# The shift unit of a graph-transformer layer moved into the last feed-forward quarter, in two groups of tiles

## The reference

```python
xn = layernorm(x)
x = x + gnn(xn) + mixer(xn)       # gnn: 4 experts of 2 graph layers; mixer: 2 attention + feed-forward layers
x = x + shift_unit(layernorm(x))  # last step, row by row:
# y = layernorm(x); hot = y > 0.5
# lo, hi, sa = first hot column of y[64:80], y[80:96], y[96:112] (0 if none)
# val = lo + 16*hi; shl = (val << sa) & 255; shr = val >> sa
# act_shl = hot[0] and hot[39];  act_shr = hot[0] and hot[40] and not hot[39]
# res = shl, shr or 0;  amp = 2 if either is active
# y[128:144] += amp * onehot(res & 15);  y[144:160] += amp * onehot(res >> 4)
```

## Time and profile before

| | us |
|---|---|
| median of 3 runs (lowest to highest) | 1983.43 (1982.74 to 1987.58) |
| the profiled execution's own time | 1988.76 |
| its span | 1986.9 |
| TensorE busy | 1815.1 |
| TensorE's last matmul ends, from the span's start | 1956.5 |
| VectorE's last instruction ends | 1981.9 |

### The profile page before, as it was taken

One profiled execution on the slowest core, in us unless ns is written; L12 is line 12 of the kernel. 1 busy time (PEld: TensorE's weight loads), 2 busy tenths in 40 slices (PEclk: granted clock), 3 DMA queues, 4 the chain that ended last, 5 costly groups with the idle time before them and its releaser, 6 DMA issues. The chain is left out here.

```text
span 1986.9 us, 26833 instructions
## 1 busy us (share of the span) xinstructions
PE 1815.1 (91%) x9484; PEld 1498.1 (75%) x9484; DVE 863.3 (43%) x1777; ACT 646.4 (33%) x1211; POOL 614.2 (31%) x503
## 2 busy tenths in 40 slices
PE   1798999999999999968999989999989998899993
PEld 1455788888888788857788867887877988778883
DVE  8996311111111146455565456222666554552236
ACT  7844211111111211015546523221365465222210
POOL 4003432323241343106321006433361210254432
PEclk9999999999999999989999999999999999999997
DMA  2168512213121567235702001011175020011102
GB/s 62 41 150 135 70 60 94 86 69 127 47 106 42 198 232 195 95 113 147 212 27 95 22 1 42 22 43 46 36 202 155 30 92 22 1 43 43 57 25 65
DMA packets 112174, 166.46 MB, mean 84 GB/s; under 512 B 42712, under 2 KB 60871, under 8 KB 111052
## 3 DMA queue, kind: packets, MB, share of 16 engines
q1 hardware_dynamic: 112067, 165.05, 28.8%
HBM read 103.24 MB, written 55.53 MB: 80 GB/s over the span
## 5 line engine op out<-in xcount | busy, mean ns | idle before, releaser
L774 PE MATMUL ps<-yT,wslot 128*128 128x500 f32 (+1 forms) x576 | 208.3, 362 | 9.5 <-ACT qpT L1790 5.9
L775 PE MATMUL ps<-yT,wslot 128*128 128x500 f32 (+1 forms) x576 | 207.3, 360 | 0.0
L776 PE MATMUL ps<-yT,wslot 128*128 128x500 f32 (+1 forms) x576 | 207.0, 359 | 0.0
L1018 PE MATMUL ps<-g,adj 125*128 125x512 f32 (+1 forms) x800 | 186.3, 394 | 1.4 <-DVEq L1153 1.2
L1018 PEld LDWEIGHTS ps<-g,adj 125*128 125x128 f32 (+1 forms) x800 | 150.2, 188 | 37.5 <-DVEq L1153 1.6
L2152 POOL TENSOR_TENSOR hidT<-qpT,hidT 128x500 fp32r<-128x500 f32 (+1 forms) x96 | 103.3, 1079 | 213.8 <-DVE hidT L1935 213.8
L1790 ACT ACTIVATE qpT<-ps,all_cols 128x500 f32<-128x500 f32 (+1 forms) x96 | 58.1, 610 | 313.8 <-PE ps L776 266.7
L2147 POOL TENSOR_TENSOR wslot<-mix_landing,wslot 128x512 fp32r<-128x512 f32 x92 | 121.8, 1354 | 115.1 <-ACT wslot L1726 115.1
L774 PE MATMUL ps<-parts,w 128*128 128x500 f32 (+1 forms) x384 | 136.0, 354 | 2.2 <-PEq L559 2.2
L775 PE MATMUL ps<-parts,w 128*128 128x500 f32 (+1 forms) x384 | 136.1, 354 | 0.0
L776 PE MATMUL ps<-parts,w 128*128 128x500 f32 (+1 forms) x384 | 136.0, 354 | 0.0
(11 more groups left out here) (295 smaller groups left out, 3686.8 us busy)
## 6 DMA issues: line engine op xcount, KB each, us to landing
mix_landing<-in_L_mix_W SPq DMA_DIRECT2D x16, 1024.0 KB, 5.1
qk_dram<-qk_parts SPq DMA_DIRECT2D x128, 125.0 KB, 2.4
g_dram<-staged SPq DMA_DIRECT2D x40, 256.0 KB, 2.0
u_dram<-staged SPq DMA_DIRECT2D x40, 256.0 KB, 2.0
g_in<-g_dram SPq DMA_DIRECT2D x40, 256.0 KB, 3.6
u_in<-u_dram SPq DMA_DIRECT2D x40, 256.0 KB, 2.7
k_stack<-qk_dram SPq DMA_DIRECT2D x8, 1250.0 KB
q_stack<-qk_dram SPq DMA_DIRECT2D x8, 1250.0 KB
```

Of the source, the lines that this page charges most:

```text
L774: nc.tensor.matmul(out, lhs_high, rhs_high, start=first, stop=False)
L775: nc.tensor.matmul(out, lhs_high, rhs_low, start=False, stop=False)
L776: return nc.tensor.matmul(out, lhs_low, rhs_high, start=False, stop=last)
L1018: last = nc.tensor.matmul(m.ps[0:counts.shape[1], t % 2, :], counts if exact else counts.bitcast(F32), part if exact else part.bitcast(F32 ...
```

## The change

The shift unit leaves its own stage and becomes part of `stage_mixer`. Its small tiles are placed in the SBUF of weight slot 1, which no product of the last quarter reads. In detail:

- The graph add of tile t leaves `add_ff`. `add_gnn(t)` follows cast number t of hidden chunks 0 and 1 in the last quarter (tiles 0 to 7); tiles 8 and 9 follow behind chunk 1, ahead of output tile 0's add.
- After hidden chunk 2 VectorE aggregates tiles 0 to 3, copies the counts, and then puts one section of the first group's work (tiles 0 to 3: norm, hits and digits, values, results, one-hot) between the adds of tiles 4, 5, 6, 7, 8 and 9. The first group (columns 0 to 511) is stored whole.
- The second group (tiles 4 to 9) goes through the same functions after the last `bn_stats`. Its columns 160 to 511 are stored when ScalarE has made them all, its columns 0 to 159 at the end.
- `ln` is made for columns 0 to 111 alone. The output itself is made in place by ScalarE: xm * (1 + rstd) - mean * rstd, one Identity per tile over all 512 columns. GpSimd's ten adds and the last add of 1600 columns are gone.
- ScalarE does a Sqrt on one column behind its last gelu, ahead of the wait for the variances.
- The arithmetic is shortened: `down` is multiplied in the compare, SHL and SHR are multiplied by the mark in the compare, integers are written by the instruction that makes the value.

The diff, cut to its core (g is the group, FINAL = ((0, 4), (4, 10)), NARROW = 112, WIDE = 160):

```diff
                             split_high(i, hidden_split(n), hT[:, 0, f, c0:c0 + cn], cn)
...
+                            if i + 1 == DEPTH and b == QUARTERS - 1 and c < 2:
+                                add_gnn(c * K + f)
+
+                    def add_gnn(t):
+                        vec.wait_ge(gnn_loaded[t % 4], stacks_loaded + 32 * (t // 4 + 1))
+                        nc.vector.tensor_tensor(xm[:, t, :], xm[:, t, :], z[:, t % 4, :], ALU.add).then_inc(m.gnn_added, 1)
...
-                                if i + 1 == DEPTH:
-                                    vec.wait_ge(gnn_loaded[t % 4], stacks_loaded + 32 * (t // 4 + 1))
-                                    nc.vector.tensor_tensor(xm[:, t, :], xm[:, t, :], z[:, t % 4, :], ALU.add).then_inc(m.gnn_added, 1)
-                                    vec.drain()
...
+                    else:
+                        add_gnn(2 * K)
+                        add_gnn(2 * K + 1)
                     vec.drain()
                     add_ff(b, 0, 4)
...
+                def final_norm(g):
+                    t0, t1 = FINAL[g]
+                    vec.wait_ge(std_made, DEPTH * 6 + g + 1)
+                    nc.vector.reciprocal(rstd[:, t0:t1], std[:, t0:t1])
+                    vec.drain()
+                    nc.vector.tensor_scalar(gain[:, t0:t1], rstd[:, t0:t1], 1.0, None, ALU.add)
+                    nc.vector.scalar_tensor_tensor(offset[:, t0:t1], mv[:, t0:t1, 0], -1.0, rstd[:, t0:t1], ALU.mult, ALU.mult)
+                    for t in range(t0, t1):
+                        nc.vector.tensor_scalar(ln[:, t, :], xm[:, t, 0:NARROW], mv[:, t, 0:1], rstd[:, t:t + 1], ALU.subtract, ALU.mult)\
+                            .then_inc(ln_ready, 1)
+                    vec.drain()
...
+                    vec.wait_ge(wide_ready, t1)
+                    v.tensor_tensor(xm[:, t0:t1, OUT:WIDE], xm[:, t0:t1, OUT:WIDE], hot[:, t0:t1].rearrange("p t a d -> p t (a d)"), ALU.add)\
+                        .then_inc(narrow_ready, 1)
+
+                final_stats(0)
+                vec.wait_ge(counts_made, 2)
...
+                add_ff(b, 4, 5)
+                final_norm(0)
+                add_ff(b, 5, 6)
+                hits(0)
+                digits(0)
+                add_ff(b, 6, 7)
+                values(0)
+                add_ff(b, 7, 8)
+                results(0)
+                add_ff(b, 8, 9)
+                put_hot(0)
+                add_ff(b, 9, T)
+                vec.drain()
+                final_stats(1)
+                final_norm(1)
+                hits(1)
+                digits(1)
+                values(1)
+                results(1)
+                put_hot(1)
```

In a group, `hits` has 2 instructions, `digits` 3, `values` 3 + 2 + 3 + 2 and `results` 1 + 1 + 1 + 2 + 1, where a plus stands for a drain; `put_hot` has 2 + 2 + 1. On ScalarE and SyncE:

```diff
+                nc.scalar.activation(gain[:, 0:1], m.eps_col[0:P, :], ACT.Sqrt)
+                act.drain()
+                for g, (t0, t1) in enumerate(FINAL):
+                    act.wait_ge(var_ready, DEPTH * 6 + g + 1)
+                    nc.scalar.activation(std[:, t0:t1], mv[:, t0:t1, 1], ACT.Sqrt, bias=m.eps_col[0:P, :]).then_inc(std_made, 1)
+                    for t in range(t0, t1):
+                        act.wait_ge(ln_ready, t + 1)
+                        nc.scalar.activation(xm[:, t, :], xm[:, t, :], ACT.Identity, bias=offset[:, t:t + 1], scale=gain[:, t:t + 1])\
+                            .then_inc(wide_ready, 1)
...
+                sp.wait_ge(narrow_ready, 1)
+                for p0, p1 in ((0, EVEN), (EVEN, P)):
+                    sp.dma_start(ov[p0:p1, 0:FINAL[0][1]], xm[p0:p1, 0:FINAL[0][1]]).then_inc(out_stored, 16)
+                sp.wait_ge(wide_ready, T)
+                for p0, p1 in ((0, EVEN), (EVEN, P)):
+                    sp.dma_start(ov[p0:p1, FINAL[1][0]:, WIDE:], xm[p0:p1, FINAL[1][0]:, WIDE:]).then_inc(out_stored, 16)
+                sp.wait_ge(narrow_ready, 2)
+                for p0, p1 in ((0, EVEN), (EVEN, P)):
+                    sp.dma_start(ov[p0:p1, FINAL[1][0]:, 0:WIDE], xm[p0:p1, FINAL[1][0]:, 0:WIDE]).then_inc(out_stored, 16)
+                sp.wait_ge(out_stored, 96)
```

More of the change, by code:

```diff
@@ L1273, in stage_mixer, with unit @@
         slots = [place(f"wslot{n}", [128, 2, K, D], F32R, (at_kp if n < 2 else at_v) + n % 2 * SLOT_BYTES) for n in range(4)]
+        MARK, SHL, LO, DIGITS, OUT = 0, 39, 64, 16, 128
+        NARROW, WIDE = LO + 3 * DIGITS, OUT + 2 * DIGITS
+        FINAL = ((0, 4), (4, T))
+        at_unit = at_kp + SLOT_BYTES
+        def unit(name, shape, dt=F32):
+            nonlocal at_unit
+            at, size = at_unit, 4
+            for n in shape[1:]:
+                size *= n
+            at_unit = at + -(-size // 32) * 32
+            assert at_unit <= at_kp + 2 * SLOT_BYTES
+            return place(name, shape, dt, at)
+        ln = unit("ln", [P, T, NARROW])
+        gain = unit("gain", [P, T])
+        offset = unit("offset", [P, T])
+        count_i = unit("count_i", [P, 2, DIGITS], I32)
+        down = unit("down", [P, 3 * DIGITS])
+        up = unit("up", [P, DIGITS])
+        first = unit("first", [P, T, 3 * DIGITS])
+        best = unit("best", [P, T, 3])
+        found = unit("found", [P, T, 3])
+        digit = unit("digit", [P, T, 3])
+        mark = unit("mark", [P, T])
+        flag = unit("flag", [P, 2, T])
+        value_i = unit("value_i", [P, T], I32)
+        shift_i = unit("amount_i", [P, T], I32)
+        shifted_i = unit("shifted_i", [P, 2, T], I32)
+        shifted = unit("shifted", [P, 2, T])
+        result_i = unit("result_i", [P, T], I32)
+        nibble_i = unit("nibble_i", [P, 2, T], I32)
+        nibble = unit("nibble", [P, 2, T])
+        amp = unit("amp", [P, T])
+        hot = unit("hot2", [P, T, 2, DIGITS])
+        counts_made, ln_ready, wide_ready, narrow_ready, out_stored = (
+            sem("counts_made"), sem("ln_ready"), sem("wide_ready"), sem("narrow_ready"), sem("out_stored"))
+        ov = out.rearrange("(t p) d -> p t d", p=P)
         rows_loaded, proj_loaded = sem("rows_loaded"), sem("proj_loaded")
@@ new lines, in hits, with digits @@
+                def hits(g):
+                    t0, t1 = FINAL[g]
+                    n = t1 - t0
+                    nc.vector.scalar_tensor_tensor(first[:, t0:t1, :], ln[:, t0:t1, LO:NARROW], 0.5,
+                                                   down[:].unsqueeze(1).to_broadcast([P, n, 3 * DIGITS]), ALU.is_gt, ALU.mult)
+                    nc.vector.tensor_scalar(mark[:, t0:t1], ln[:, t0:t1, MARK], 0.5, None, ALU.is_gt)
+                    vec.drain()
+                def digits(g):
+                    t0, t1 = FINAL[g]
+                    nc.vector.tensor_reduce(best[:, t0:t1, :], first[:, t0:t1, :].rearrange("p t (a d) -> p t a d", d=DIGITS), X, ALU.max)
+                    for s in range(2):
+                        nc.vector.scalar_tensor_tensor(flag[:, s, t0:t1], ln[:, t0:t1, SHL + s], 0.5, mark[:, t0:t1], ALU.is_gt, ALU.mult)
+                    vec.drain()
@@ new lines, in results @@
+                def results(g):
+                    v = nc.vector
+                    s = slice(*FINAL[g])
+                    v.tensor_scalar(shifted_i[:, 0, s], shifted_i[:, 0, s], 255, None, ALU.bitwise_and)
+                    vec.drain()
+                    v.tensor_tensor(shifted[:, :, s], shifted_i[:, :, s], flag[:, :, s], ALU.mult)
+                    vec.drain()
+                    v.tensor_tensor(result_i[:, s], shifted[:, 0, s], shifted[:, 1, s], ALU.add)
+                    vec.drain()
+                    v.tensor_scalar(nibble_i[:, 0, s], result_i[:, s], 15, None, ALU.bitwise_and)
+                    v.tensor_scalar(nibble_i[:, 1, s], result_i[:, s], 4, None, ALU.logical_shift_right)
+                    vec.drain()
+                    v.tensor_copy(nibble[:, :, s], nibble_i[:, :, s])
+                    vec.drain()
@@ new lines, in put_hot @@
+                def put_hot(g):
+                    v = nc.vector
+                    t0, t1 = FINAL[g]
+                    n = t1 - t0
+                    for a in range(2):
+                        v.tensor_tensor(hot[:, t0:t1, a, :], up[:].unsqueeze(1).to_broadcast([P, n, DIGITS]),
+                                        nibble[:, a, t0:t1].unsqueeze(2).to_broadcast([P, n, DIGITS]), ALU.is_equal)
+                    vec.drain()
+                    for a in range(2):
+                        v.tensor_tensor(hot[:, t0:t1, a, :], hot[:, t0:t1, a, :], amp[:, t0:t1].unsqueeze(2).to_broadcast([P, n, DIGITS]), ALU.mult)
+                    vec.drain()
+                    vec.wait_ge(wide_ready, t1)
+                    v.tensor_tensor(xm[:, t0:t1, OUT:WIDE], xm[:, t0:t1, OUT:WIDE], hot[:, t0:t1].rearrange("p t a d -> p t (a d)"), ALU.add)\
+                        .then_inc(narrow_ready, 1)
@@ L2217, in _ @@
                         split_rows(i + 1, 1)
[L2221 to L2276, removed]
```

119 lines of the change are left out of this document (32 added, 87 removed).

## The result

The changed kernel takes 1972.45 us (median of 4 runs, 1971.35 to 1973.55) against 1983.09 us (4 runs): ratio 0.9933, interval 0.9906 to 0.9960. It is faster, by 10.6 us. The forecast was 1968.2 us, range 1965.0 to 1973.5, so the result lies inside the range, near its upper end.

A forecast was written before the change was run, and what follows sets the result against it. Bound: TensorE's last tile, then one VectorE chain and the stores behind it. Terms -15.6 + 0.1 + 0.3 = -15.2 us gave 1973.6 against 1988.76 profiled; with the median 5.3 below, 1968.2 us, range 1965 to 1973.5.

The forecast's parts named there:

- What bounds the end: Behind TensorE's last tile: only that tile's arrival and the VectorE chain with stores behind it count; 30.4 us before.
- The chain: VectorE behind the last matmul: ends at 1966.1 against 1981.87, 15.8 us earlier.
- six normalizations: Second group's norm on VectorE: 0.24 us each, 0.15 from start to start, 1.0 plus drain 0.08.
- results: Five levels of small VectorE instructions for six tiles behind the last matmul: 1.38 us.
- The stores: Span's end: narrow store queues behind the wide one, so the transfer ends last, at 1971.3; by the chain alone 1970.0.
- the wait at tile 0's add: Last quarter, three graph adds behind the last cast may delay tile 0's add; priced 0.3 us between ends 0 and 2.9.
- A wait of 0.8: TensorE's wait at tile 0 if one add stretched by 1.1 us and splits came 0.8 late.
- the prediction's own signs of being wrong: Last quarter: a `z` add over 1.5 us with a TensorE wait, clock under 1, tile 9's add later than 1957, among others.
- The first rival: Wait at tile 0 of 2.9 us and lower clock costing 1.4: -11.2 us, 1972.2; chance 0.14.
- The sections between the adds: First group's work between tiles 4 and 9: sum 6.4 us against 6.2 of room, price 0.1.
- The table load: ScalarE's load of 1.28 us moves behind the last gelu, covered by 18 us idle; without cover 1.3 us.
- The median: Whole kernel: the 5.3 us between profiled execution and median of runs carried over, giving 1968.2 us.

The follow-up runs named there:

- e9: e5 with the normalization of 112 columns replaced by one compare with mean + 0.5 x std for the group; 1967.96 us, median of 6.
- e11: e9 with the last wide store cut into three parts (tiles 4 to 6, 7 and 8, 9); 1969.23 us, median of 6.
- e6: Changed kernel with the graph adds put back into each tile's add; 1973.31 us, median of 4.
- e4: Changed kernel with all ten tiles in one group behind the last tile, wide columns stored in two halves; 1973.53 us, median of 5.
- e7: Kernel before with only the graph adds moved as in the change; 1983.19 us, one run.
- e10: e4 without the early Sqrt on one column; 1980.15 us, one run.
- e3: Changed kernel without the store of columns 160 to 511 of tiles 4 to 9; 1968.42 us, one run.
- e5: Changed kernel with graph adds of tiles 8 and 9 moved behind tiles 1 and 2, last wide store in two parts; 1968.72 us, median of 5.
- e8: Changed kernel without the early Sqrt on one column; 1973.22 us, one run.

## Why the prediction was right, and what was mis-sized

**What bounds the end** was as argued: TensorE at full clock, then one VectorE chain, then stores. -15.2 was forecast for the profiled execution, -14.35 came in the stretches that the change touches.

**The chain** was forecast at 9.6 from the last matmul to VectorE's end and measured 10.28. By pieces, forecast and measured: aggregates to the reciprocal 0.89 and 0.88; to the first normalization 0.47 and 0.42; hits and digits 1.31 and 1.28; values 1.52 and 1.44; one-hot 1.38 and 1.37. The prices of small instructions from the earlier trace rows held to 0.1. Two terms were mis-sized. The **six normalizations** were 1.67 to the next instruction instead of 1.08: they start 0.25 apart, where the line between 30 and 512 columns gave 0.15. That line took its lower end from an instruction with fixed scalars, while a normalization has two scalars per row; this is the likely reason, but no run changes the scalars alone. The **results** were 1.64 instead of 1.38, because of 0.42 us idle ahead of `result_i` for which the trace has no releaser. The idle time belongs to a place in VectorE's program and not to that instruction: counting every VectorE record, those for semaphores included, it stands ahead of record 3406 in all ten traces with two groups, which is `result_i` in seven of them, `nibble_i` in e9 and e11 (0.43 too) and `amount_i` in e6 (0.22). The traces of before, e4, e7 and e10 end ahead of that record and have no such gap. It isn't SyncE's issue of the wide store that begins just before it, since e3, which has no wide store, has the gap too (0.43). What VectorE waits for there stays open.

**The stores**: "what ends last is the transfer, not VectorE". e3 and e5 show it, 1.2 us. Forecast 5.2 behind VectorE, measured 4.93; because VectorE was later than forecast, less of the wide store was left. The Trainium skill (DMA: Bandwidth & Descriptors, Anatomy of one DMA) has a fit, 2.0 us plus bytes over 436 GB/s, for a DMA issued from GpSimd. These stores are issued from SyncE, and the fit doesn't carry over: for 0.48 MB it gives an estimated 3.1 us, and e5 has 3.7 with a nearly empty queue.

**The last quarter.** The step that failed here was the choice of 0.3 for the wait at tile 0's add, "for chunk 1's inputs come 2.7 us apart here". "A wait of 0.8" was what one stretched add and late splits would make; 0.6 of wait and 0.85 in all came, at the place that was named, before output tile 2 and behind three graph adds. The Trainium skill's rule (SBUF — State Buffer, SBUF: two separate sides), that VectorE with two SBUF inputs and a GpSimd reader exclude each other, fits: two adds beside the weight part took 1.79 instead of 0.69, each behind a GpSimd instruction. The distance of the inputs didn't prevent it. The last cast ended 1.3 us later than in the kernel before, and from the first of the three adds to tile 0's add it took 2.85 instead of the 2.34 counted: 1.8 late in all, against a leeway of 1.1. Two of the prediction's own signs of being wrong came with it: adds of `z` over 1.5 us with a TensorE wait behind them, and, by the 0.85 of A, tile 9's add at 1957.4 on the time axis of the kernel before (1954.29, and 3.07 by which this last quarter began sooner), where "later than 1957" was named. The first rival's condition held (a wait), but not its price: 0.6 instead of 2.9 and no lower clock. That the first median lies next to this rival's 1972.2 is chance. The sections between the adds cost 6.3 in all, as forecast to 0.1 (the norm section 1.55 instead of 1.24, the others less); tile 9's add found VectorE waiting.

**The table load** was priced at 0 by the right cover and the wrong mechanism: I had it move with the Sqrt that the change adds, and e8 and e10 show that it goes ahead of the wait by itself. "Without it, 1.3 us" is refuted for this block.

**The median.** The forecast was 4.2 us too low (1968.2 against 1972.45), and the step that failed most was the last: 5.3 carried over whole from the profiled execution. The median of three runs of before was 1983.43, while 46 give 1985.2. From 1985.2 the stretches' 14.35 gives 1970.8. So of the 4.2, some 1.7 is the low median of before, 0.85 what the stretches came short, and the remaining 1.7 the spread ahead of the last quarter, which the prediction didn't price. That the median still lies in the range is partly luck: the upper part of the range stood for a wait of 2.9 us and a lower clock, and neither came.

## What to carry to other kernels

Work that follows the bounding engine's last instruction can go between its last products, as long as each section fits the leeway per product; count first what already stands there and move it away (here the graph adds, worth nothing alone and 3.3 us as room). Moved work has to be spread as well: three adds in a row ahead of the first product's add cost what one per product doesn't. When the chain is short, look at the queue behind it: sending the bulk in two parts gave 1.25 us, and after that a chain 0.9 us shorter gave nothing. Effects of a few us are read from stretches of the traces; medians of a few runs here were off by as much.

## What the runs showed that was not expected

- ScalarE's table load runs ahead of the semaphore wait of the instruction that needs it, right behind the previous one (over 17.4 us early in e10).
- A VectorE instruction with two scalars per row costs 0.25 us from start to start at 112 columns, as much as two to three small ones; one compare of 288 columns took 0.45 in e9.
- VectorE idles for 0.42 us at one place of its program, whatever instruction stands there (0.22 in e6).
- SyncE's issue of two stores takes 0.84 to 0.94 us with an empty queue, 1.68 while a store of 1.06 MB is going out, and 2.55 in e4 right behind a store of 0.88 MB.
- Executions of one kernel on one core lie up to 12 us apart, and the two traces furthest apart (8.3 us) differ by 24 us of half clock ahead of the last quarter and by 0.02 us in it.
